# Attention in half steps, with values behind each maxima pair and outputs kept transposed

## The reference

```
qkv = layernorm(x) @ w_qkv              # 16 heads of 16, 4 batches of 1024 tokens
attn = softmax(q @ k^T / 4)             # [1024 x 1024] per head and batch
y = attn @ v                            # back to [4, 1024, 256]
x = x + y @ w_proj
```

## Time and profile before

| | us |
|---|---|
| median of three runs | 1647.42 |
| the profiled execution | 1646.13 |
| its span, first to last instruction | 1643.3 |
| stages before attention, to its first scores matmul | 519.3 |
| attention | 519.3 to 1275 |
| projection, routing, experts | 1275 to 1643.3 |

### The profile page before, as it was taken

The page is one execution under the profiler, slowest core; times in us unless marked ns, Lnnn a source line. Parts: engine busy times, 40 slices in busy tenths (PEclk is TensorE's granted clock), DMA queues, the critical chain, the costliest instruction groups (busy, mean ns, idle before and its releaser), DMA issues. The chain is left out here.

```text
span 1643.3 us, 28821 instructions
## 1 busy us (share of the span) xinstructions
PE 1493.4 (91%) x10138; PEld 861.5 (52%) x10138; DVE 1283.4 (78%) x2433; ACT 1007.5 (61%) x1713; POOL 199.6 (12%) x376
## 2 busy tenths in 40 slices
PE   7688998979999999999999999999998869999997
PEld 7565665656554333333333333333333738999997
DVE  6899999845666888888888888888880767777773
ACT  3699999934334777777777777777775633222221
POOL 3011111132110000000000000000000451222222
PEclk9799999999999999999999999999997979999999
DMA  3300110027957223322233222322301657566561
GB/s 109 90 8 14 50 44 21 23 88 262 292 188 200 69 65 77 78 67 59 71 72 79 59 59 72 72 51 55 75 17 52 201 210 244 209 212 212 202 201 61
DMA packets 148700, 176.25 MB, mean 107 GB/s; under 512 B 71744, under 2 KB 106560, under 8 KB 148560
## 3 DMA queue, kind: packets, MB, share of 16 engines
q1 hardware_dynamic: 143152, 160.95, 33.0%
q0 software_dynamic: 4432, 13.24, 2.0%
q10 hardware_dynamic: 976, 0.24, 0.1%
HBM read 120.75 MB, written 53.43 MB: 106 GB/s over the span
## 5 line engine op out<-in xcount | busy, mean ns | idle before, releaser
L1691 ACT ACTIVATE at_p<-at_pst 128x512 f32<-128x512 f32 x1024 | 539.4, 603 | 199.2 <-PE at_pst L1803 199.1
L1704 DVE TENSOR_REDUCE at_mx<-at_pmx 128x2 f32<-128x1024 f32 x490 | 583.3, 1222 | 90.0 <-PE at_pmx L1781 85.6
L1803 PE MATMUL at_pst<-at_q,at_k 50*128 50x512 f32 x1024 | 368.5, 447 | 5.8 <-ACT at_p L1691 3.5
L1781 PE MATMUL at_pmx<-at_k,at_q 48*128 48x512 f32 x980 | 267.4, 461 | 51.5 <-DVE at_mx L1704 51.5
L1803 PEld LDWEIGHTS at_pst<-at_q,at_k 50*128 50x128 f32 x1024 | 159.8, 188 | 290.7 <-ACT at_p L1691 255.1
L1813 PE MATMUL at_pacc<-at_p,at_v 128*32 128x512 f32 x2048 | 277.1, 613 | 2.1
L878 PE MATMUL ws_pA<-ident,ws_A 128*128 128x128 f32 x1088 | 151.1, 285 | 24.0 <-ACT ws_A L660 21.3
L1781 PEld LDWEIGHTS at_pmx<-at_k,at_q 48*128 48x128 f32 x980 | 117.9, 185 | 101.9 <-DVE at_mx L1704 99.0
L878 PEld LDWEIGHTS ws_pA<-ident,ws_A 128*128 128x128 f32 x1088 | 121.1, 145 | 83.7 <-ACT ws_A L660 38.9
L2362 DVE STREAM_TRANSPOSE ex_zr<-ex_row 32x64 f32<-32x64 f32 x608 | 143.1, 235 | 15.2 <-DMA ex_row<-scratch_routed 7.4
L2402 PE MATMUL ex_pH<-ex_zT,ex_w 128*128 128x128 f32 x1248 | 145.8, 275 | 2.3 <-ACT ex_zT L2339 2.3
(11 more groups left out here) (278 smaller groups left out, 1546.6 us busy)
## 6 DMA issues: line engine op xcount, KB each, us to landing
ex_w<-in_L_ffn_w SPq DMA_DIRECT2D x39, 1024.0 KB, 5.5
at_q<-scratch_qs SPq DMA_DIRECT2D x192, 64.0 KB, 2.8
at_k<-scratch_ks SPq DMA_DIRECT2D x192, 64.0 KB, 2.9
ex_row<-scratch_routed SPq DMA_DIRECT2D x39, 258.0 KB, 5.0
scratch_qs<-gp_split SPq DMA_DIRECT2D x16, 512.0 KB, 4.1
scratch_ks<-gp_split SPq DMA_DIRECT2D x16, 512.0 KB, 3.6
scratch_v<-gp_v SPq DMA_DIRECT2D x8, 1024.0 KB, 5.5
at_v<-scratch_v SPq DMA_DIRECT2D x32, 256.0 KB, 3.6
```

Source lines behind the costliest of these rows:

```text
L1691: a.activation(pt[k // 2 % 4][:, k % 2, :], pst[bank(w, k)][:], ACT.Exp).then_inc(exped, 1)
L1704: v.reduce_max(mx[u % 2][:].rearrange("p (h n) k -> p h n k", h=2)[:, :, j // 2, j % 2], slot(w, j)[:], AX.X).then_inc(taken, 1)
L1781: last = nc.tensor.matmul(slot(w, j)[:, h, :], att.rows(qst[u], h, ROWS)[:, nt * P:(nt + 1) * P], att.rows(kst[u], h, ROWS)[:, kh * HALF:( ...
L1803: nc.tensor.matmul(pst[bank(w, k)][:], att.rows(kst[u], h, FULL)[:, t * P:(t + 1) * P], att.rows(qst[u], h, FULL)[:, p * HALF:(p + 1) * HA ...
```

## The change

`attention` is rewritten; the arithmetic is the same.

- A unit has 16 **half steps**, one per tile of keys and half of the queries. In each TensorE issues one maxima pair, two scores matmuls, and the values of two half steps before. Values now have four matmuls of 256 queries (two heads by two quarters); the first half step of a unit is taken together with the second (512 queries).
- Maxima are turned by VectorE: `tops` takes the larger of the two halves, splits high and low part (128x16 each), and transposes a 128x32 tile in blocks of 32. The transposed rows lie in four groups of partitions, so `store_top` takes 16 DMAs of 8 partitions by 32 elements, where it took four of 8 partitions by 128.
- Outputs are not turned. ScalarE copies `pacc` to `at_oe` behind the third Exp of a unit. SyncE folds the four denominator rows to 128x16 (`fold`, 4 DMAs), VectorE inverts them (`invert`, at half step 7), SyncE writes them to scratch memory and waits until they have landed, then reads them back broadcast over 16 partitions (`spread`, 1 and 4 DMAs), GpSimd multiplies (`normalise`, 128x512), SyncE stores to a transposed `YT` (`store`, 4 DMAs).
- The projection behind reads `YT` directly; its turns and copies are gone (`first.load`, `project`). The last unit's `spread` and `store` move into `project_and_route`.
- The loads of v count on the same semaphore as those of q and k.

The core of the diff:

```diff
-    ORDER = "SMSEMSSV"
+    STEPS = 2 * BT
+    TURN = 2 * att.TURN
+    BANKS, SLOTS, BUFS = 3, 2, 4
+    LAG = 2
+    COPY = 2
+    INVERT = 7
...
+            def unit(w):
+                if w:
+                    outputs.fold(sp, w - 1)
+                    if w + 3 < UNITS:
+                        sp.wait_ge(pv, w * STEPS)
+                        load(w + 3)
+                if w % 2:
+                    load_w2(w)
+                elif 0 < w <= 2 * E:
+                    pad(w // 2 - 1)
+                if w:
+                    outputs.spread(sp, w - 1)
+                if w + 1 < UNITS:
+                    att.store_top(sp, w + 1)
+                if w:
+                    outputs.store(sp, w - 1)
+                if w == UNITS - 2:
+                    load_first()
...
+    def fold(self, sp, w):
+        rows = P // self.PARTS
+        sp.wait_ge(self.oed, w + 1)
+        for part in range(self.PARTS):
+            at = part * 2 * DK + DK
+            sp.dma_start(self.den[w % 2][part * rows:(part + 1) * rows, :],
+                         self.oe[w % 2][at:at + 1, :].rearrange("o (a b) -> o a b", b=self.FOLD)).then_inc(self.den_in, 16)
...
+    def spread(self, sp, w):
+        sp.wait_ge(self.inverted, w + 1)
+        sp.dma_start(self.rden[w, :].rearrange("(a b) -> a b", b=self.FOLD), self.inv[w % 2][:]).then_inc(self.inv_out, 16)
+        sp.wait_ge(self.yd, w)
+        sp.wait_ge(self.inv_out, (w + 1) * 16)
+        for part in range(self.PARTS):
+            at, n = part * 2 * DK, L // 2
+            sp.dma_start(self.rd[at:at + DK, :],
+                         self.rden[w:w + 1, part * n:(part + 1) * n].to_broadcast([DK, n])).then_inc(self.rd_in, 16)
...
+    def store_top(self, eng, w):
+        eng.wait_ge(self.topT, w + 1)
         for h in range(2):
             for n in range(2):
-                at = h * self.BASE + self.ROWS + n
-                eng.dma_start(self.qst[u][at:at + 1, :].bitcast(F32).rearrange("o (t n) -> o t n", t=BT),
-                              self.top2[u % 2][h * BT:(h + 1) * BT, n, :].bitcast(F32)).then_inc(self.rows_in, 16)
+                at, c = h * self.BASE + self.ROWS + n, n * self.PIECES + h * BT
+                row = self.qst[w % self.RING][at:at + 1, :].bitcast(F32).rearrange("o (t i j) -> o t i j", t=BT, j=self.Q)
+                for i in range(P // self.Q):
+                    eng.dma_start(row[:, :, i, :], self.turned[w % 2][i * self.Q + c:i * self.Q + c + BT, :]).then_inc(self.rows_in[w % 2], 16)
...
             def out(w):
-                a.wait_ge(pv, PV0 + (w + 1) * BT)
-                a.wait_ge(oT, w)
-                a.copy(oe[:], pacc[:]).then_inc(oed, 1)
+                a.wait_ge(pv, (w + 1) * STEPS)
+                if w >= 2:
+                    a.wait_ge(outputs.y_out[w % 2], w // 2 * outputs.MOVES)
+                a.copy(oe[w % 2][:], pacc[:]).then_inc(oed, 1)
...
+            for w in range(UNITS):
+                pe.wait_ge(att.rows_in[w % 2], (w // 2 + 1) * att.TOP_ROWS)
+                for s in range(STEPS):
+                    n = w * STEPS + s
+                    m = beside(w, s)
+                    if m:
+                        maxima(*m)
+                    for h in range(2):
+                        scores(n, h)
+                    if n >= LAG:
+                        values(n - LAG)
```

More of the change, by code:

```diff
@@ L1528, in attention @@
     paired, taken = sem("at_paired"), sem("at_slot_taken")
-    oed, oT, yd, rd = (sem("at_" + n) for n in ("acc_out", "outT", "y", "rden"))
+    pO = [pmx[n][:].rearrange("p x n -> p (x n)").rearrange("p (t c) -> p t c", c=C) for n in range(2)]
     with nc.Block() as block, nc.allow_non_contiguous_dma(reason="per-channel vectors"):
[L1532 to L1592, removed]
@@ L1594, in _, with beside, nth, load @@
+        def beside(w, s):
+            ahead, j = (1, EARLY + s) if s < TURN else (2, s - TURN)
+            return (w + ahead, j) if w + ahead < UNITS else None
+        def nth(w, j):
+            return (w - 1) * STEPS + j - EARLY
         @block.sync
         def _(sp):
[L1596 to L1603, removed]
+            def load(w):
+                b, pair, u = w // (H // 2), w % (H // 2), w % RING
@@ L1607, in load @@
                 sp.dma_start(vst[u][:].rearrange("p t h d -> p t (h d)"),
[L1608 to L1622, removed]
+                             dr["v"][b * L:(b + 1) * L, pair * (4 * DK):(pair + 1) * (4 * DK)].rearrange("(t p) n -> p t n", p=P)).then_inc(ld[u], 16)
@@ L1744, in _, with maximum @@
[L1744 to L1751 removed]
+            def maximum(w, j):
+                n = nth(w, j)
+                dve.wait_ge(paired, n + 1)
+                v.reduce_max(mx[w % 2][:].rearrange("p (h n) k -> p h n k", h=2)[:, :, j // 2, j % 2], pmx[n % SLOTS][:], AX.X).then_inc(taken, 1)
@@ L1752, in _ @@
+            for w in range(UNITS):
+                for s in range(STEPS):
+                    m = beside(w, s)
+                    if m:
+                        maximum(*m)
+                    if s == INVERT and w:
+                        outputs.invert(v, w - 1)
+                    if s == TURN - 1 and m:
+                        dve.wait_ge(taken, nth(*m) + 1)
+                        att.tops(v, w + 1)
             dve.wait_ge(first.outed, 1)
@@ L1876, in projection_weights @@
+            for n in range(UNITS * STEPS - LAG, UNITS * STEPS):
+                values(n)
 def projection_weights(sb, io):
@@ L2249, in _ @@
                     gate(pp)
-                if i is not None and i + 1 < CHUNKS:
-                    turn(i + 1)
                 if prev is not None:
```

406 lines of the change are left out of this document (157 added, 249 removed).

## The result

The changed kernel takes 1957.39 us (median of four runs, 1941.0 to 1962.25) against 1642.56 for the kernel before on the same chip: a ratio of 1.19, 95% interval [1.18, 1.20]. Forecast were 1860 us and a range of 1735 to 1935. The direction and the place were right, the size was not: by the profiled executions' own times 309 us were lost (1955.48 against 1646.13) where 214 were forecast, and the median lies 22 us above the range.

What follows compares the result with a forecast made beforehand. SyncE's DMA queue was to bound attention: unit 1 at 550.3 us, 28 units at 30.3, two at 29.6, 31 for the last, 368.3 behind it and 2.8 outside the span give 1860 us, range 1735 to 1935.

Steps and rivals of the forecast that it cites:

- the two loops: Attention unit: SyncE's line from copy to last row's landing, 30.3 us; split maxima, 16 row issues and landing, 29.8 us.
- the last unit with the change of stage: End of attention: 10 us cold, 11 warm, 10 for projection matmuls, last values, copy, fold and stage change; 31 us.
- the loop is 30.3 us: SyncE's queue in a unit with loads: copy at 5.6 us, then fold, loads, w2 or pad, spread, rows, landing.
- with 6 us cold: Attention unit's start: two and a half half steps at the low clock, then 7.5 warm, before the split maxima.
- both are nearly tied: SyncE reaches its wait for the split maxima at t + 18.2 us; they are ready at t + 17.5.
- the two signs of being wrong: Attention units: copies 21 us apart, or SyncE's queue waiting for VectorE in each unit by more than a microsecond.
- the prediction's own sum: SyncE's loop in a warm unit: copy 3.1, fold and loads 7.9, w2 0.45, spread 2.3 and 1.9, rows 10.9, landing 1.4.
- those 2.4: Clock's cost per unit with loads: two cold half steps at the head delay the copy; the clock-stays-up rival counted 28 x 2.4.
- The queue keeps up: Rival: SyncE issues everything within the engines' 20.5 us per attention unit; 1562 us, chance 0.06.
- The clock stays down through the unit: Rival: ten half steps of an attention unit at 2.45 us, unit 37.8 us; 2085 us, chance 0.07.
- Short runs issue like loads: Rival: the 16 row DMAs cost 0.46 us each, not 0.68, 3.5 us less in both loops; 1755 us, chance 0.13.
- The engines' 20.5: Attention unit by engines alone: sixteen half steps, TensorE 19.5 us, VectorE 19.9, about 20.5 us with hand-overs.

Runs made afterwards that it cites:

- hot2: The changed kernel with eight matmuls that compute nothing at each unit's head, one per second row DMA of SyncE: 1886.13 us, ratio 1.145 to the kernel before.
- both: The changed kernel with maxima rows in 4 DMAs instead of 16, and fold, spread and store of the outputs on GpSimd's queue: 1588.05 us, ratio 0.962.
- bothfull: As both, with the values of a tile of keys taken in one group of 512 queries every second half step: 1659 us, ratio 1.006.

## Why the prediction was wrong

**Right: the place and the kind.** SyncE's in-order queue became the bound, with the two loops as told. The parts of the sum outside the loop of 28 units came out as follows: unit 1 starts at 549.5, forecast 550.3; the two units without loads take 30.5 and 30.8 from start to start, forecast 29.6; the last unit with the change of stage runs from 1555.8 to 1587.5, 31.7, forecast 31; the stages behind take 366, forecast 368.3. Their errors cancel to less than 1 us. Prices per issue held but for one: 0.46 a load, 0.68 a row. That the rows keep the price of 8 partitions although each run is a quarter as long is seen in 512 issues with a median of 632 ns, against 635 in the earlier trace rows.

**Wrong: "the loop is 30.3 us".** It measured 33.75, and 28 x 3.45 is 97 us: all of the miss.

- The step that failed is "with 6 us cold" and, with it, "both are nearly tied" at 29.8, which lets SyncE's queue wait for VectorE nowhere. I took the length of the cold stretch from one place at the start of the stage. In the loop the clock stood low for 11 to 22 us of dense matmuls (954.4 to 976 in the unit shown, 989.3 to 1000 in the next). A cold half step measured 2.16, less than my 2.45 (the copy ends at t + 5.05, forecast 5.6), but there were ten of them in the unit shown and five in the next, where I had two and a half. So the inverse came late and the split maxima at up to t + 22.6 (forecast 17.5), behind which 12.2 stand. SyncE's waits for VectorE are 73.5 us over 24 units (53.1 and 20.4), 3.1 a unit, where the sum has none. A wait for VectorE of more than a microsecond a unit is one of the two signs of being wrong that the prediction names.
- fold: 2.52 for four, 0.59 each by the median, where I took the load's 0.46: 0.7 us a unit.
- Smaller terms go both ways. In the unit shown (34.9 us) the waits are 3.2 and 1.4, fold is 0.7 and loads, w2 and rows 0.6 over the forecast, and the copy, the reads and the two landings are 1.5 under it.

**A second error, which the first one hid.** Held warm, a unit should have been 27.9 by the prediction's own sum; `hot2` has 31.5. Fold is 0.7 of that, the landing of the inverses 1.3 (3.3 behind an issue of 0.34 to 0.43, forecast 2.3 with the issue), loads 0.9 (median 6.9 for the 13, forecast 6.0), and SyncE's counting up 0.4, which belongs to the experiment. The rest, 0.3, stays open. From `hot2` to the kernel as changed the low clock adds 2.3 us, or 2.7 without the counting up, and the forecast had 2.4 for it. That agreement is luck: those 2.4 stood for a later copy, and what came was a wait for VectorE, under which part of the loads and of the landing disappeared.

The Trainium skill, "TensorE: Matmul & The Clock Gate", section "HAM oscillation — how this bites in real kernels", describes a kernel in which each block of matmuls starts at the low clock because it waits for a DMA in front of it. The traces agree in this, with 0.70 over attention after the change and 1.00 in `hot2`, whose heads are filled.

**The rivals.** "The queue keeps up" is false as built, and true once 12 issues are saved and 13 moved (`both`). "The clock stays down through the unit" was given 0.07 and 37.8 us; it is what happens in part, in about half of the units (9 or more cold half steps), and should have moved the forecast rather than stood beside it. "Short runs issue like loads" is false. The engines' 20.5 was 0.8 too low, and it is TensorE's half step of 1.24 and its two stalls that make the 21.27 (`both`).

The Trainium skill, "DMA: Bandwidth & Descriptors", section "Issuing engines are not separate DMA queues", calls the cost of starting a DMA usually small beside the DMA. For the rows of maxima the traces do not agree: issuing one takes 0.63 us for 1 KB, and the last of a unit had landed 1.07 us behind its issue (988.21 to 989.28). In the loop there are 496 of them, and they set its pace. The measurement decides.

## What to carry to other kernels

Count the issues on an in-order DMA queue that lie between the event that frees them and the wait that needs the last of them; a queue that is idle for half of a period has no room there if its idle time lies elsewhere. Price an issue by its shape, not by its bytes. And where a loop gets a stall at its head, don't take the cost of the clock from one recovery seen elsewhere: the low clock delays the results that the stall waits for, so the two feed each other, and a range should hold the case that it lasts for the whole period.

## What the runs showed of the hardware that was not expected

The low clock can last. In the changed kernel's attention, 27 idle stretches of 3 to 11 us at the heads of units were followed by it. TensorE got the full clock back after 5 us of work in three cases, after 10 to 16 in eleven, after 19 to 29 in ten, and after 33, 55 and 57 us in the other three. In the profiled run of `bothfull` it stood at 0.50 through the first eight units, with TensorE busy all the time:

```profile
560.00:850.00 290.00, 290.00 (x1022) 103.83 (x1018) 163.16 (x192) 136.53 (x263) 63.01 (x112) 0.50 0.18 49
850.00:1200.00 350.00, 318.75 (x1908) 120.16 (x1904) 300.54 (x358) 253.32 (x492) 117.67 (x210) 1.00 0.29 74
```

Those units took 36.4 us each, the later ones 23.5. No other kernel here showed this in its profile, and what brought it on is not known.

GpSimd's queue issued the loads of q and k at 0.48 us each and the outputs' DMAs at 0.49 to 0.56, about as SyncE's did. The load of v, with 128 partitions, took it 0.94, where SyncE's took 0.42. A transpose of 32x32 on VectorE takes 0.200 and one of 128x32 0.21: the price is per instruction here.
